# Moving the routing-row copy of a mixture-of-experts kernel to the GpSimd DMA queue, one expert ahead

## What is computed

```python
x = x + attn(layernorm(x))                 # 8 heads of 64, softmax over 2048 keys
xf = layernorm(x)                          # S x 1024
shared_out = silu(xf @ sgw.T) * (xf @ suw.T) @ sdw.T      # hidden size 2048
topk_idx, w = route(xf)                    # 4 of 16 experts, weights sum to 1
combine = zeros(S, 16); combine[s, topk_idx] += w
g = einsum('sc,ech->esh', xf, gate_w)      # hidden size 256 per expert
u = einsum('sc,ech->esh', xf, up_w)
hw = silu(g) * u * combine.T[:, :, None]
routed = einsum('esh,ehc->sc', hw, down_w)
x = x + shared_out + routed
```

## Time and profile before

| | |
|---|---|
| median of 2 runs | 11818.72 us |
| the two runs | 11679.14 and 11958.29 us |
| the profiled execution | 11614.01 us |
| its span on the slowest core (core 2) | 11612.5 us |
| spans of the eight cores | 11580.9 to 11612.5 us |
| TensorE busy, share of the span | 7983.6 us, 69% |
| VectorE busy | 4141.0 us, 36% |
| ScalarE busy | 2070.3 us, 18% |
| GpSimd busy | 600.0 us, 5% |

### The profile page before, as it was taken

How to read it: one execution, slowest core, us unless ns; L and a number is a source line. 1 busy time by engine, 2 the same in 40 slices (tenths; PEclk the granted TensorE clock), 3 DMA queues, 4 the chain that set the end, 5 groups by cost and what they waited for, 6 DMA issues and landing times.

```text
span 11612.5 us, 114552 instructions; the slowest of 8 cores (11580.9 to 11612.5 us)
## 1 busy us (share of the span) xinstructions
PE 7983.6 (69%) x40456; PEld 4143.7 (36%) x40880; DVE 4141.0 (36%) x7140; ACT 2070.3 (18%) x2428; POOL 600.0 (5%) x482
## 2 busy tenths in 40 slices
PE   4677558679467755867936775577793677557779
PEld 2344323234234432323413443233341444323334
DVE  4455432220345543222044554322204455432220
ACT  1222221100122222110012223211001222321100
POOL 0000110000000011000000001100000000110000
PEclk9555579889655557878965555788896555578889
DMA  2000025334200002533420000253342000035334
GB/s 48 1 1 1 24 60 84 62 59 127 50 1 1 1 26 58 84 62 66 122 49 1 1 1 29 57 86 57 66 122 49 1 1 1 30 58 87 57 67 120
DMA packets 773148, 544.63 MB, mean 47 GB/s; under 512 B 541143, under 2 KB 676311, under 8 KB 772588
## 3 DMA queue, kind: packets, MB, share of 16 engines
q0 software_dynamic: 302528, 167.79, 11.4%
q1 hardware_dynamic: 75820, 268.82, 6.3%
q10 hardware_dynamic: 394240, 100.67, 4.1%
HBM read 536.95 MB, written 167.77 MB: 61 GB/s over the span
## 4 chain that ended last, share of the span: by engine, by line
PE 61%; DVE 20%; DMA 6%; issue 5%; ACT 4%; POOL 3%; DVEq 1%; SPq 0%; ACTq 0%; POOLq 0%
PE ps L1130 11%; DVE arena L619 9%; PE ps L1056 9%; PE ps L552 8%; PE ps L1061 8%; PE ps L611 6%; PE ps L638 5%; DMA arena<-arena 4%; PE ps L965 4%; PE ps L969 4%; PE ps L435 2%; POOL arena L732 1%; DVE arena L647 1%; POOL arena L728 1%; DVE arena L503 1%
## 5 line engine op out<-in xcount | busy, mean ns | idle before, releaser
L619 DVE CAST arena<-ps 128x512 bf16<-128x512 f32 x2048 | 1416.4, 692 | 1000.5 <-PE ps L611 818.5
L566 ACT ACTIVATE arena<-ps,arena 128x2048 bf16<-128x2048 f32 x512 | 1053.2, 2057 | 2703.3 <-PE ps L552 2702.7
L1130 PE MATMUL ps<-arena 128*128 128x512 bf16 x6020 | 1327.8, 381 | 77.1 <-DMA arena<-h_cache 70.6
L1056 PE MATMUL ps<-arena 128*128 128x512 bf16 x4040 | 1066.3, 410 | 168.1 <-DVE arena L1043 161.7
L552 PE MATMUL ps<-arena 64*128 64x512 bf16 x2048 | 936.7, 612 | 275.3 <-DVE arena L647 273.6
L1061 PE MATMUL ps<-arena 128*128 128x512 bf16 x3984 | 988.5, 389 | 6.7 <-issue 1.1
L611 PEld LDWEIGHTS ps<-arena 128*128 128x128 bf16 x8192 | 829.8, 146 | 450.1 <-issue 450.1
L611 PE MATMUL ps<-arena 128*128 128x128 bf16 x8192 | 964.3, 312 | 27.9 <-DVE arena L601 27.9
L1130 PEld LDWEIGHTS ps<-arena 128*128 128x128 bf16 x6144 | 602.7, 98 | 802.2 <-issue 82.6
L1083 DVE TENSOR_TENSOR arena<-ps,arena 128x512 bf16<-128x512 f32 x512 | 354.0, 691 | 1429.2 <-ACT arena L1075 1429.2
L638 PE MATMUL ps<-arena 128*64 128x128 bf16 x4096 | 523.8, 308 | 361.5 <-DVE arena L619 361.5
(11 more groups left out here) (144 smaller groups left out, 5521.6 us busy)
## 6 DMA issues: line engine op xcount, KB each, us to landing
h_cache<-arena SPq DMA_DIRECT2D x192, 512.0 KB
arena<-h_cache ACTq DMA_DIRECT2D x64, 1536.0 KB, 11.2
arena<-x SPq DMA_DIRECT2D x128, 512.0 KB, 3.5
x_cache<-arena SPq DMA_DIRECT2D x64, 512.0 KB, 2.9
arena<-gw POOLq DMA_DIRECT2D x64, 512.0 KB, 7.5
arena<-uw POOLq DMA_DIRECT2D x64, 512.0 KB, 10.2
arena<-dw POOLq DMA_DIRECT2D x64, 512.0 KB, 6.0
arena<-x_cache SPq DMA_DIRECT2D x64, 512.0 KB
```

The source lines that it names most:

```text
L566: return sc.activation(P_t[:], ps[:, cb:cb + 2048], AF.Exp, bias=rs_t[:, 16 + hidx:17 + hidx], scale=consts[:, CSCL:CSCL + 1], accum_out=r ...
L619: return v.tensor_copy(Pt_t[:, 512 * q4:512 * (q4 + 1)], ps[:, cb + 512 * q4:cb + 512 * (q4 + 1)])
L1056: tn.matmul(ps[:, gc:gc + 512], wg_buf[:, e % 2, kc, 128 * hc:128 * (hc + 1)], lnF[:, kc, 512 * tb:512 * (tb + 1)], start=(kc == 0), stop= ...
L1130: li = tn.matmul(ps[:, base + 512 * nh:base + 512 * (nh + 1)], h_ring[:, t % 2, kc, :], wd_sb[:, kc, 512 * nh:512 * (nh + 1)], start=(kc = ...
```

## The change

The copy of the routing row is issued by GpSimd in place of SyncE, counts a semaphore of its own (SD), and stands ahead of the same expert's weight loads in GpSimd's list. Its waits are as they were: the last L1083 of expert e-2, which read the same buffer, and for the first two experts the end of stage C. The spreading matmuls wait for SD in place of SA2. Besides, the ring of the x tiles is reset at the end of a sequence to the last readers of the two row buffers (which lie in the same memory) in place of the counts of all engines.

```diff
@@ -34,14 +34,14 @@
     def __init__(self):
         self.ops = {e: [] for e in self.ENGINES}
         self.cnt = {"T": 0, "V": 0, "S": 0, "G": 0, "SA": 0, "SG": 0,
-                    "SC": 0, "SA2": 0, "SG2": 0, "SC2": 0}
+                    "SC": 0, "SA2": 0, "SG2": 0, "SC2": 0, "SD": 0}
 
     def emit(self, eng, fn, waits=(), inc=None):
         waits = [(s, v) for (s, v) in waits if v and v > 0]
         for s, v in waits:
             assert v <= self.cnt[s], (s, v, self.cnt[s])
         after = None
-        if inc in ("SA", "SG", "SC", "SA2", "SG2", "SC2"):
+        if inc in ("SA", "SG", "SC", "SA2", "SG2", "SC2", "SD"):
             if self.cnt[inc] > 0:
                 waits = [(inc, self.cnt[inc])] + waits
         elif inc in ("V", "S", "G"):
@@ -1002,6 +1002,12 @@
         v_cb = None
         cb_free = {0: (("V", v_combF),), 1: (("V", v_combF),)}
         for e in range(E):
+            cb_t = cB_sb if e % 2 == 0 else cb2_sb
+            wl = list(cb_free[e % 2])
+            if e < 2:
+                wl.append(("V", v_C_end))
+            sa_cst = EMIT("G", dma_g(cb_t[0:1, :], combF[e:e + 1, :]),
+                          waits=wl, inc="SD")
             wl = wgr.waits(e)
             if e < 2:
                 wl += [("T", t_shared_end), ("V", v_C_end), ("G", g_C_end)]
@@ -1020,13 +1026,6 @@
                     sdw.rearrange("(kc p) f -> p kc f", p=128)[:, 4 * e:4 * (e + 1), :]),
                     inc="SG")
 
-            cb_t = cB_sb if e % 2 == 0 else cb2_sb
-            wl = list(cb_free[e % 2])
-            if e < 2:
-                wl.append(("V", v_C_end))
-            sa_cst = EMIT("SY", dma_sy(cb_t[0:1, :], combF[e:e + 1, :]),
-                          waits=wl, inc="SA2")
-
             def f(tn, e=e, cb_t=cb_t):
                 li = None
                 for nb in range(4):
@@ -1036,7 +1035,7 @@
                                    start=True, stop=True)
                 return li
             t_cbb = EMIT("T", f,
-                         waits=[("SA2", sa_cst)]
+                         waits=[("SD", sa_cst)]
                          + ([("V", v_cb)] if v_cb else []), inc="T")
 
             def f(v, cb_t=cb_t):
@@ -1162,8 +1161,9 @@
         endbar = sched.bar()
         deps = tuple((k, endbar[k])
                      for k in ("T", "V", "S", "SA", "SC", "SA2", "SC2"))
-        for r in (xr, lr, tpr, p0r, z1r, hr, x1er, x2r, swr, wgr, x1wr, scr1r):
+        for r in (lr, tpr, p0r, z1r, hr, x1er, x2r, swr, wgr, x1wr, scr1r):
             r.reset(*deps)
+        xr.reset(cb_free[0][0], cb_free[1][0])
 
     sa_final = sched.now("SA")
     sa2_final = sched.now("SA2")
@@ -1183,11 +1183,12 @@
         nc.semaphore("semSA2") as semSA2,
         nc.semaphore("semSG2") as semSG2,
         nc.semaphore("semSC2") as semSC2,
+        nc.semaphore("semSD") as semSD,
         nc.Block() as blk,
     ):
         sems = {"T": semT, "V": semV, "S": semS, "G": semG, "SA": semSA,
                 "SG": semSG, "SC": semSC, "SA2": semSA2, "SG2": semSG2,
-                "SC2": semSC2}
+                "SC2": semSC2, "SD": semSD}
 
         @blk.tensor
         def _(eng):
```

## The result

The changed kernel took 11201.74 us in the median of 12 runs (11007.18 to 11693.02). The kernel before, run beside it on the same chip, took 11952.51 in the median of 10 (11610.79 to 12131.41). The ratio is 0.9505, with a 95% interval of 0.9422 to 0.9587: about 5% faster.

A forecast was written before the change was run, and what follows sets the result against it. TensorE was taken to stand still 64 times, 14.4 us each, for the routing row queued behind a store. Shrinking 60 stops to 4.6 us saves 588 of 11614.0 us, giving 11026, named as 11050; range 10890 to 11250.

The forecast's parts named there:

- The stop: At each change of expert TensorE's stop shrinks from 14.4 to 4.6 us, 3.8 of them idle.
- The first experts: The four sequences' first experts gain next to nothing, as uw decides there; 60 stops shrink, not 64.
- POOL's order: On POOL's queue gw goes out some 2 us later behind the row copy; margin 7 us, cost nothing.
- Rivals B and C: B: weight loads bind experts 1 to 3, 11092 us, chance 0.05; C: row late on POOL's queue, 12334 us, 0.02.
- The clock after a stop: TensorE's matmuls after each stop still run at low clock, costing 1.9 us a stop as before; no gain taken.
- rival A: TensorE's clock stays up across the shorter pause, 114 us more go, 10912 us; chance 0.15.
- The x ring: The new reset at a sequence's end changes nothing, since the barrier still holds the first x load; cost and gain zero.
- The sum: Over the whole kernel, 60 x (14.4 - 4.6) = 588 us off the profiled 11614.0 gives 11026 us.
- the one from the sum to the runs: Profiled time lay 65 us below the faster run, 205 below the median; hence 11050 named, range top 11231, rounded to 11250.
- rival D: Denser expert matmuls pull the clock down on all cores; at half the low-level loss 11909 us; chance 0.02.

The follow-up runs named there:

- e1: The kernel before with the row copy kept on SyncE's queue but issued one expert ahead; lowest 11057.11 us, median 11374.94.
- e2: The changed kernel, but for experts 1 to 15 the row copy on POOL's queue waits for the previous expert's last VectorE instruction; ratio to before 0.9718.
- e8: The kernel before with the loads of gw and uw waiting for the row, which stays late on SyncE's queue; lowest 11522.71 us, median 11661.31.
- e4: The changed kernel with the old reset of the x ring; lowest 11449.17 us of 4 runs.
- e3: The kernel before with only the new reset of the x ring; 11890.17 and 12007.43 us, ratio to before 1.022.
- e6: The changed kernel without the weight-load entry (SG) in the barrier at the top of the loop; lowest 10928.41 us, median 11186.03.
- a2: The changed kernel run once more, unaltered; lowest 11405.72 us, median 11601.41 of 5 runs.
- e5: The changed kernel with the next expert's row spread and copied back in the middle of the expert before; lowest 10822.56 us, median 11209.84.
- e7: The changed kernel with e5 and e6 joined, and gw and uw of expert 0 loaded during the shared expert; lowest 10595.13 us, median 10825.49.
- e9: e7 with expert 0's row copy moved behind the shared expert's first eight loads; run again, lowest 10536.57 us, ratio to the kernel before 0.9047.

## Why the prediction was wrong, and where it was right

**The stop.** Right. 4.6 us by the sum, 4.7 measured; 3.8 us idle, 3.7 measured; the wait is for L1043's counterpart behind VectorE's tail. e1 shows that the reason given (the place in SyncE's list) is the whole one for the 60 stops, and e2 and e8 that over half of the row's own way came from gw and uw ahead of it, which the prediction had not asked about.

**The first experts.** Right that they gain next to nothing: uw still decides, 46.2 us of wait in four. The forecast for L1056's idle time was 240 us, 228 of them for the copy; 223.6 were measured for the copy, and the rest of the 273.4 is the wait for uw, which before was mostly hidden behind the row.

**POOL's order.** Right at nothing: gw comes about 2 us later, and no expert but the first waits for weights. Rivals B and C are out, the row lands in 3.1 us.

**The clock after a stop.** Right: it falls as before (407 and 383 ns against 410 and 389), rival A did not come. What the means give, 36 us of duration, would cover the 19 us by which the lowest run lies below the sum; on core 2 of e4, which had none of the 0.81, they are 409 and 380.

**The x ring.** Right at zero (e3, e4), and for the reason given: the wait was the barrier's for the weight loads (e6).

**The sum.** 11026 us against 11614 is a ratio of 0.9494; measured is 0.9505, and the lowest run is 11007. The saving was put at 588 us, and the lowest runs are 604 apart.

**The step that failed is the one from the sum to the runs, and with it rival D.** For its number the prediction went 24 us above the sum, of the 65 by which the faster of two runs lay above the profile, and for the top of the range 205. That offset was mis-sized: beside the changed kernel the kernel before has a median of 11952.51, 338 us above its profiled execution. At the measured ratio this level is 0.9505 x 11952.51 = 11361 us, above the range that ended at 11250; and the forecast as a ratio, 11050 / 11818.72 = 0.935, set a number near the profile against a median that is not, and so lies outside the measured interval. That the median of the twelve runs, 11201.74, lies inside the range, and that 11201.74 / 11952.51 = 0.937 is near the forecast, is luck: it depends on how much of the lower clock these executions met. The next five of the same kernel (a2) had a median of 11601.41 beside 11858.87, which is 0.978.

The cause of the level is the granted clock. The prediction saw one stretch at 1.00 and one profile without another level, gave a lower clock under dense matmuls 0.02, and took it for something that the change might bring. By its own sign ("a clock below 1.00 within the long stretches") that rival is there, at 0.81 and not at the half clock that its price was worked out for. The profile after has it in the shared expert's matmuls, which the change doesn't touch (core 4; the last three figures of the first row are the granted clock, the DMA share and GB/s):

```profile
1855.00:1880.00 25.00, 24.35 (x92) 9.78 (x91) 4.12 (x6) 3.58 (x6) 1.01 (x2) 0.81 0.05 22
```

```profile
1855.10 2.27 PE L969 MATMUL ps<-arena 128*128 128x512 bf16 x8
```

Eight matmuls take 2.27 us in place of 1.89. The lower clock doesn't need the change: e3, which is the kernel before but for the x reset, has it in its down projection (409 ns), and in the runs of the kernel before the mean granted clock of a core goes down to 0.657, where it is 0.71 in the lowest runs. So it is a term of the level of the runs for either kernel, and it belonged into the step from profile to median, not among the rivals. Whether the change makes it larger is open: over all sets the executions lie above the lowest of their kernel by 282 us in the mean for the kernel before (48 of them) and by 386 for the changed one (17), and single ones by 0 to 760 and 0 to 690. The rule that the prediction had cited for it, from the Trainium skill ("TensorE: Matmul & The Clock Gate", Part 1, a die held at 13/16 under dense matmuls on three cores), agrees with the 0.81 of these rows; what the prediction's trace refuted was only that it is always so.

## What to carry to other kernels

A transfer that stands behind a store in an engine's list inherits the store's wait: look in the timeline at what each small DMA on the path waited for in its queue and what it needed, and issue it where the latter is ready. When a wait is taken away, ask what its neighbours in the lists (here VectorE's tail, the PSUM copy, the barrier's other entries) make of the time; what was left here, 4.7 us a stop with 1.9 us of low clock behind it, was worth 321 us more (e5), over half of what the change gave. A sum made on one profiled execution gives a ratio between executions at the same clock. Before you name a time in microseconds, look at how far the kernel's runs lie above its profile, and at more than two of them.

## What the runs showed of the hardware

- TensorE's granted clock has a level of 0.81 between its usual two in these eight-core programs. Some profiled executions have none of it on any core (the kernel before, e7, e9 when it was run again), others up to 3260 us on a core (a2), and it can differ between the two dies: in e4 cores 0 to 3 have none and cores 4 to 7 have 2310 to 2570 us. It was seen in the changed kernel and in variants with the old stops (e3, e8) and without stops (e5). What sets it off in one execution and not in the next is not shown.
- A 4 KB copy within on-chip memory takes 2.5 us from issue to use when no weight load is issued just ahead of it, on SyncE's queue as on POOL's (e8, e2), and 8.0 us with two weight loads issued 1 to 2 us ahead of it. A small transfer pays for the large ones ahead of it even when they are on another engine's queue.
- A stop of TensorE with 3.7 us idle lets the clock fall to its low level just as the old one with 10.6 us idle did: the eight matmuls behind it take 3.16 us and not 1.89.
